# Attention in front of a feed-forward block: the probability-value products in two groups of eight heads in place of four groups of four

## The reference, cut to what matters

```python
q, k, v = (x @ w.T for w in (wq, wk, wv))             # 16 heads of 8 features
attn = einsum('bhqd,bhkd->bhqk', q, k) / sqrt(8) - slope[h] * abs(key - query)
attn = softmax(attn, axis=-1)
out = einsum('bhqk,bhkd->bhqd', attn, v)              # the products in question
x = layernorm(x + out @ wo.T + bo)
x = layernorm(x + ffn(x))
```

## Time and profile before

| | |
|---|---|
| median of 3 runs | 962.63 us (962.04 to 964.39) |
| span of the profiled execution | 961.6 us |
| TensorE busy | 911.5 us, 95% |
| VectorE busy | 737.4 us, 77% |
| ScalarE busy | 654.9 us, 68% |
| GpSimd busy | 140.6 us, 15% |

### The profile page before, as it was taken

The page is one execution under the profiler, slowest core; times in us unless marked ns, Lnnn a source line. Parts: engine busy times, 40 slices in busy tenths (PEclk is TensorE's granted clock), DMA queues, the critical chain, the costliest instruction groups (busy, mean ns, idle before and its releaser), DMA issues. The chain is left out here.

```text
span 961.6 us, 24138 instructions
## 1 busy us (share of the span) xinstructions
PE 911.5 (95%) x6914; PEld 724.1 (75%) x6914; DVE 737.4 (77%) x3039; ACT 654.9 (68%) x1168; POOL 140.6 (15%) x213
## 2 busy tenths in 40 slices
PE   1899999999999999999999996899999999999995
PEld 1677778787787877878778774688888888888883
DVE  5789898888888888888888873667766777776764
ACT  4277676676666766667666764677777777777773
POOL 3002112121211212112121132000010000000101
PEclk9799999999999999999999998899999999999998
DMA  6244443444434344443444420001111111111001
GB/s 176 79 134 114 129 116 109 125 107 129 114 111 126 105 125 117 113 122 106 126 118 116 124 80 20 25 25 45 33 33 33 33 44 42 34 39 37 23 23 44
DMA packets 72307, 80.60 MB, mean 84 GB/s; under 512 B 8208, under 2 KB 68368, under 8 KB 69200
## 3 DMA queue, kind: packets, MB, share of 16 engines
q1 hardware_dynamic: 71392, 77.28, 28.9%
q0 software_dynamic: 880, 2.88, 1.1%
HBM read 45.53 MB, written 33.55 MB: 82 GB/s over the span
## 5 line engine op out<-in xcount | busy, mean ns | idle before, releaser
L614 DVE CUSTOM_DVE_ANT_0 scored<-ps_a,corner_rows 128x256 f32<-128x256 f32 x1024 | 376.1, 418 | 21.7 <-PE ps_a L371 8.6
L524 ACT ACTIVATE probs<-ps_b 128x512 f32<-128x512 f32 x512 | 301.7, 599 | 128.7 <-PE ps_b L362 125.8
L371 PE MATMUL ps_a<-qk_stack 126*128 126x256 f32 x1024 | 255.4, 333 | 17.2 <-DMA qk_stack<-qk_scratch 15.1
L383 PE MATMUL ps_b<-qk_stack 128*128 128x256 f32 x1024 | 209.5, 286 | 2.3 <-ACT probs L524 2.1
L371 PEld LDWEIGHTS ps_a<-qk_stack 126*128 126x128 f32 x1024 | 162.3, 197 | 47.1 <-issue 29.7
L383 PEld LDWEIGHTS ps_b<-qk_stack 128*128 128x128 f32 x1024 | 159.3, 191 | 6.5 <-ACT probs L524 3.8
L848 ACT ACTIVATE gelu_f<-ps_r,sc 128x512 f32<-128x512 f32 x128 | 88.3, 690 | 79.9 <-PE ps_r L789 72.4
L396 PE MATMUL ps_o<-probs,v_aug 128*32 128x256 f32 x2048 | 137.0, 385 | 0.4 <-ACT probs L524 0.4
L362 PE MATMUL ps_b<-corner_sb,idb_sb 128*128 128x158 bf16 x512 | 125.3, 245 | 0.0
L786 PE MATMUL ps_r<-g1h,h_hi 128*128 128x512 f32 x256 | 102.6, 401 | 2.0 <-DVE g1l L913 1.9
L786 PE MATMUL ps_r<-g2h,h_hi 128*128 128x512 f32 x256 | 102.8, 401 | 0.0
(11 more groups left out here) (99 smaller groups left out, 1366.8 us busy)
## 6 DMA issues: line engine op xcount, KB each, us to landing
qk_stack<-qk_scratch SPq DMA_DIRECT2D x64, 384.0 KB
qk_scratch<-x_parts SPq DMA_DIRECT2D x32, 512.0 KB, 3.0
qk_scratch<-x_parts SPq DMA_DIRECT2D x32, 256.0 KB, 3.3
xT_sb<-in_xT SPq DMA_DIRECT2D x32, 128.0 KB, 2.1
x_sb<-in_x SPq DMA_DIRECT2D x32, 128.0 KB, 2.1
x_scratch<-x_sb SPq DMA_DIRECT2D x32, 128.0 KB, 1.7
x_in<-x_scratch SPq DMA_DIRECT2D x32, 128.0 KB, 2.1
x_res<-x_scratch SPq DMA_DIRECT2D x32, 128.0 KB, 2.1
```

Source lines behind the costliest of these rows:

```text
L371: mm = pe.matmul(ps[:, qb * SEQ:(qb + 1) * SEQ], q_stack[par][0:KA, h, qb * P:(qb + 1) * P], k_stack[par][0:KA, h, :], start=(qb == 0), st ...
L383: pe.matmul(ps[:, kb * SEQ:(kb + 1) * SEQ], k_stack[par][:, h, kb * P:(kb + 1) * P], q_stack[par][:, h, :], start=(kb == 0), stop=False, s ...
L524: nc.scalar.activation(probs[:, k % HALF, :], ps_b[k % 2][:], ACT.Exp, scale=slope[k]).then_inc(exp_done, 1)
L614: ins = nc.vector.tensor_tensor_reduce(scored[:, k % 2, qb, :], ps_a[A_BANK[k]][:, qb * SEQ:(qb + 1) * SEQ], corner_rows[:, qb, :], -1.0, ...
```

## The change

The products come in two groups of eight heads a batch. Groups 0 and 1 both stand in slot 9; groups 2 and 3 both stand in slot 1 of the next step, still ahead of `turn_max`. Slots 5 and 13 hold none. `probs` grows from 8 to 16 heads (from 16 to 32 KB a partition), and ScalarE waits for the products in slots 0 and 8 only, each time for products of the batch before. The instructions of a group, its operands and PSUM targets stay as they are.

```diff
-PV_AT = (5, 9, 13)
+PV_AT = 9
...
-        probs = sb("probs", [P, HALF, BLK * SEQ])
+        probs = sb("probs", [P, HEADS, BLK * SEQ])
...
                         mm = pe.matmul(ps_o[VCOLS * g:VCOLS * (g + 1), j % 2, :],
-                                       v_aug[par][:, kb, h, :], probs[:, h % HALF, kb * SEQ:(kb + 1) * SEQ],
+                                       v_aug[par][:, kb, h, :], probs[:, h, kb * SEQ:(kb + 1) * SEQ],
                                        start=(kb == 0), stop=(kb == BLK - 1), skip_group_check=True)
...
                     if live(t, BATCH):
                         add_corner(ps_b[k % 2]).then_inc(scores_b, 1)
-                        if k in PV_AT:
-                            pv(t, s, PV_AT.index(k))
+                        if k == PV_AT:
+                            pv(t, s, 0)
+                            pv(t, s, 1)
                     if k == PE_AT["last pv"] and live(t - 1, BATCH):
+                        pv(t - 1, 1 - s, 2)
                         pv(t - 1, 1 - s, 3)
                     if k == PE_AT["turn max 1"] and live(t, BATCH):
                         wait(pe, m_lo, t * 2 + 1)
...
                 for k in range(HEADS):
                     if live(t, BATCH):
                         wait(act, scores_b, t * HEADS + k + 1)
-                        if k % GROUP == 0:
-                            wait(act, pv_done, t * 4 + k // GROUP - 1)
-                        nc.scalar.activation(probs[:, k % HALF, :], ps_b[k % 2][:], ACT.Exp,
+                        if k % HALF == 0:
+                            wait(act, pv_done, t * 4 - 2 + k // HALF * 2)
+                        nc.scalar.activation(probs[:, k, :], ps_b[k % 2][:], ACT.Exp,
                                              scale=slope[k]).then_inc(exp_done, 1)
```

## The result

The changed kernel takes 990.93 us (median of 4 runs, 989.57 to 992.43) against 963.41 us before in the same comparison: ratio 1.0301, 95% interval 1.0276 to 1.0325, slower by 3.0%. The forecast was 984.6 us, 2.3% slower, by two waits on VectorE. Time and span of one execution differ by 1.8 us here (990.92 and 989.1).

The account below looks back on a forecast made before the run. TensorE was taken to set the pace. Per step, -0.60 from joints plus stalls of 0.77 and 0.61 gave +0.78 us: +22.6 over 29 steps, -0.6 at the ends, so 984.6 us; own range 979 to 992, stretched down to 966.

Parts of the forecast that it names:

- two waits on VectorE: TensorE stalls in slots 4 to 6 and 13 to 1, +0.77 and +0.61 us a step.
- What a group and a joint cost: TensorE's products: a group costs 1.16 us, joining two saves 0.30; two joints a step give -0.60 us.
- What moves: Slot 1: `turn_max` and what follows come 0.86 us later; VectorE idles about 1.5 in front of `mrow_lo`.
- First wait: Slots 4 to 6: `turn_o` 0 waits for VectorE's `qk lo` to free its PSUM bank, +0.77 us a step.
- Second wait: Slot 13 to next slot 1: head 1 waits for VectorE to free head 14's bank, +0.61 us a step.
- Other waits: Head 0's row maxima land level with TensorE and ScalarE's further `probs` heads are free: nothing added.
- Sum: A step changes by -0.60 + 0.77 + 0.61 = +0.78 us, to 17.93.
- At the ends: First and last two steps gain up to 0.6 us each, the tail grows 0.86; together about -0.6.
- The total: Whole run +22.0 us: profiled execution 961.6 to 983.6 us, median 984.6.
- TensorE alone setting the pace: Rival: the VectorE waits don't bind, a step is 16.55 us, 944 us, up to 955; chance 0.08.
- Only one wait binds: Rival: `turn_o` doesn't wait, the slot 13 wait stays; +0.1 to +0.2 us a step, 966 to 969; chance 0.09.

Follow-up runs that it names:

- turn_first: Changed kernel with `turn_max` of the second eight heads put ahead of the two products of slot 1; 1000.49 us, ratio 1.0399.
- join_01: Changed kernel with group 2 back in slot 13, so only groups 0 and 1 are joined, in slot 9; 981.22 us, ratio 1.0186.
- res_later: Changed kernel with VectorE's residual and statistics one slot later, in 14 and 15; 980.43 us, ratio 1.0192.
- join_23: Changed kernel with group 0 back in slot 5, so only groups 2 and 3 are joined, in slot 1; 973.91 us, ratio 1.0117.
- last_four: Changed kernel, but the last batch with four separate groups in the slots of before; 988.98 us, ratio 1.0294.
- probs_16: Kernel before in its order, with `probs` of 16 heads and ScalarE's waits in slots 0 and 8 only; 962.27 us, ratio 0.9997.
- pair_01_v: Changed kernel, only groups 0 and 1 joined (not in last batch), queries/keys in slot 3, output turns in 7 and 8, values in 5; 956.3 us, ratio 0.9941.
- turn_o_later: Changed kernel with the turns of the output one slot later (7 and 8), their normalising in 8 and 9; 985.25 us, ratio 1.0242.
- pair_23: Changed kernel, only groups 2 and 3 joined, queries and keys in slot 3, residual and statistics in 14 and 15; 964.69 us, ratio 1.0032.
- both_pairs: Changed kernel with queries and keys in slot 3, output turns in 7 and 8, residual and statistics in 14 and 15; 964.89 us, ratio 1.0032.

## Why the prediction was right or wrong

- **What a group and a joint cost.** Right: 0.30 a joint forecast, 0.29 measured, no gap in the joined group (1.87 for 1.86). The 0.215 for a round was read a little short: the rows have rounds 0.24 and 0.21 apart; the second group of a pair added 1.87 - 1.00 = 0.87 for four rounds.
- **What moves.** Right in kind: VectorE idles in front of `mrow_lo` (1.10 after 0.63), and by turn_first its place in front of `mrow_lo` costs nothing. It is less than the forecast 1.5, because VectorE comes to slot 1 later than it did.
- **First wait.** Right; 0.77 forecast, 0.86 measured in the step shown and 0.84 on average. VectorE's way was as long as said (2.79 for 2.78), the release took 0.13 and 0.06 in turn in place of 0.05. It stands alone in join_01.
- **Second wait.** Right; 0.61 forecast, 0.51 measured in the step shown and 0.55 on average. It is taken away by res_later, alone; join_23 does not isolate it.
- **Other waits.** Here a term was left out. I looked at the row maxima and found them level; they held TensorE in no steady step. The transfer next to them, the stacked heads that come back behind `qk lo`, I did not price. It costs about 0.6 a step in join_23 and shows no wait in the steady steps of the full change, but in step 3, where the transfers run late, it held TensorE once:

```profile
110.48 0.50 PE L371 MATMUL ps_a<-qk_stack 126*128 126x256 f32 x2 [1.97 <-DMA qk_stack<-qk_scratch]
```

  The same step in last_four showed 0.5 and in turn_first 0.9, in the kernel before none. But probs_16, in the old order, also stood 0.93 us in front of head 0 there (put down to VectorE), and its step 3 took 18.37. So this step differs between executions of either order, and how much of its loss the change made is open.
- **Sum.** The step was 17.93 forecast and 17.94 measured. That it fits to 0.01 is partly luck: the first wait was 0.07 larger than forecast and the second 0.06 smaller, and the forecast started from 17.15 where the mean step before was 17.13.
- **At the ends.** This is the step that failed: the term of about -0.6 us for the first step, the last two and the tail, "the first step and the last two gain up to 0.6 each". Measured: step 0 +0.13, step 30 +0.51, step 31 +3.33, together +4.0; the tail's 0.86 did not show (equal to 0.2 us behind step 31). Step 30 begins with the second wait (0.62 at head 1), and leaving the group out of its slot 13 gave back only 0.63 of 1.15. For step 31 the term took the gain of the joints and priced no wait against it. But already in the kernel before TensorE stood for 2.1 of 15.5 us there, for exponentials, and ScalarE, busy for only 10.7 us, stood for TensorE's scores and for a transfer. In the changed kernel the granted clock fell as well, which is about 2.5 of the 3.33 and stood nowhere in the prediction.
- **The total.** Steps 1 to 29 gave 25.9 for the forecast 22.6; of the difference 2.5 are step 3 and 0.7 the 0.03 a step. With 4.0 at the ends, -2.25 at the start and -0.1 behind step 31 this makes 27.5 in place of 22.0. The start's -2.25 is no effect of the change and hid part of the miss. Another 0.8 us of the miss in time is the base: the forecast put the median 1.0 above the span, and it stands 1.8 above.
- **The rivals.** TensorE alone setting the pace was wrong for this order, but its price of a joint was right: pair_01_v gets it for one pair. "Only one wait binds" had the second wait alone, at +0.1 to +0.2 a step; turn_o_later comes nearest to it, with +0.45, and join_01 is the first wait alone, at +0.55.

Left open: why the clock falls in step 31 of some runs and not of others, how much of step 3's loss is the change's, and whether it is the transfer that keeps pair_23 and both_pairs from their full gain.

## What to carry to other kernels

An engine that is busy all the time can still be the pace-maker with others only 0.4 us behind it: before work is taken out of one of its slots, follow each wait across that slot and subtract. A block of work has two values, its own cost and the wait that it covers; four groups of 1.16 us each covered chains that two groups of 1.9 us elsewhere did not. Price the first and last passes of a pipeline by what each engine waits for there, be it another engine or a transfer, and look at the granted clock there too.

## What was not expected

- A 128x16 transposing matmul costs 0.03 us right behind a group of products in column quarters and about 0.3 us right ahead of it (347.02 to 347.05, against 2.34 and 2.07 for the whole).
- A release from VectorE to TensorE took 0.06 us in two places (362.32 to 362.38, and in turn_first); at L409 it was 0.06 and 0.13 in turn, from step to step.
- The granted clock fell to 1.2 GHz inside attention's last step in the changed kernel (0.65 in the window from 600 to 605 us), 0.45 us into a stand of 1.68 us, and stayed at 2.4 GHz through that step in turn_first and last_four. At the lower clock a joined group took 3.20 us in place of 1.93.
